# Slot mixture: ScalarE's copy of the turned dispatch weights placed before the combination exponential and the copy of the normalised slots

## What is computed

```python
# h: [16 batches, 192 tokens, 192], phi: [64 experts, 16 slots, 192]
xn = unit(h)                                   # normalised tokens
logits = einsum('bmd,npd->bmnp', xn, phi)
dispatch = softmax(logits, over the tokens m)  # a slot's weights over tokens
combine  = softmax(logits, over the slots np)  # a token's weights over slots
slots = einsum('bmnp,bmd->bnpd', dispatch, h)
slots = layernorm(slots) * ln_g[n] + ln_b[n]
y = gelu(slots @ w1[n] + b1[n]) @ w2[n] + b2[n]
h = h + einsum('bmnp,bnpd->bmd', combine, y)
```

## Time and profile before

| | |
|---|---|
| median of 3 runs | 2569.57 us |
| the runs | 2563.82, 2569.94, 2569.57 us |
| the profiled execution | 2563.13 us, its span 2561.2 us |
| mean granted clock of TensorE | 0.942 of full |
| slot stages (`first`, three `both`), from the first logits to the last copy of rows | 1904 to 1983, 2054 to 2142, 2211 to 2297, 2366 to 2454 us |

### The profile page before, as it was taken

How to read it: one execution, slowest core, us unless ns; L and a number is a source line. 1 busy time by engine, 2 the same in 40 slices (tenths; PEclk the granted TensorE clock), 3 DMA queues, 4 the chain that set the end, 5 groups by cost and what they waited for, 6 DMA issues and landing times. The chain is left out here.

```text
span 2561.2 us, 52598 instructions
## 1 busy us (share of the span) xinstructions
PE 2327.5 (91%) x18199; PEld 2047.2 (80%) x18199; DVE 1322.8 (52%) x3939; ACT 870.8 (34%) x2148; POOL 517.4 (20%) x616
## 2 busy tenths in 40 slices
PE   9968999997994899997999879999787999999997
PEld 9957999996873789996888667777557888888986
DVE  3663333335997211113888635655577264472744
ACT  2411222224881233332333213433344343342430
POOL 1223322322432444431222110000021010010100
PEclk9979999998995899999999867999889999999999
DMA  3124455611102686662000000000002633527265
GB/s 117 29 64 134 143 163 156 181 53 45 51 25 63 198 239 207 205 177 59 20 19 1 10 4 6 7 7 9 12 15 63 178 95 103 167 56 201 73 160 157
DMA packets 234545, 235.02 MB, mean 92 GB/s; under 512 B 29736, under 2 KB 214942, under 8 KB 234270
## 3 DMA queue, kind: packets, MB, share of 16 engines
q1 hardware_dynamic: 220638, 203.56, 28.5%
q0 software_dynamic: 11520, 27.54, 3.4%
q10 hardware_dynamic: 2240, 1.99, 0.3%
HBM read 277.77 MB, written 35.45 MB: 122 GB/s over the span
## 5 line engine op out<-in xcount | busy, mean ns | idle before, releaser
L572 PE MATMUL f_pg<-f_vxT,f_w 128*128 128x128 f32 x2112 | 260.7, 278 | 3.1 <-DVE f_vxT L642 3.1
L572 PEld LDWEIGHTS f_pg<-f_vxT,f_w 128*128 128x128 f32 x2112 | 256.1, 195 | 4.6 <-DVE f_vxT L642 4.6
L584 PE MATMUL f_po<-f_wd,f_hid 128*128 128x192 f32 x1440 | 254.3, 326 | 1.2 <-DVE f_vout L668 0.7
L584 PEld LDWEIGHTS f_po<-f_wd,f_hid 128*128 128x128 f32 x1440 | 231.2, 190 | 2.0 <-issue 1.7
L545 POOL DMA_INDIRECT f_answers<-f_vout,f_to_row x120 | 118.5, 987 | 422.8 <-DVE f_vout L666 250.6
L653 DVE TENSOR_TENSOR f_hid<-f_silu,f_pg 128x128 f32<-128x128 f32 x336 | 81.8, 284 | 207.1 <-ACT f_silu L621 191.8
L621 ACT ACTIVATE f_silu<-f_pg 128x128 f32<-128x128 f32 x336 | 78.5, 277 | 292.5 <-PE f_pg L578 272.7
L626 ACT ACTIVATE f_hid<-f_pg,f_b 128x128 f32<-128x128 f32 x384 | 106.3, 375 | 196.0 <-PE f_pg L578 196.0
L578 PE MATMUL f_pg<-f_vxT,f_wr 64*128 64x128 f32 x2112 | 151.1, 285 | 0.0
L2565 POOL TENSOR_TENSOR s_small<-s_small,s_half 128x2 f32<-128x2 f32 x64 | 44.4, 693 | 504.6 <-DVE s_small L2892 504.6
L578 PEld LDWEIGHTS f_pg<-f_vxT,f_wr 64*128 64x128 f32 x2112 | 128.0, 188 | 14.7 <-issue 0.4
(11 more groups left out here) (412 smaller groups left out, 4854.0 us busy)
## 6 DMA issues: line engine op xcount, KB each, us to landing
f_wd<-in_L_ffn_W SPq DMA_DIRECT2D x64, 576.0 KB
f_wd<-in_L_ffn_WdT SPq DMA_DIRECT2D x56, 576.0 KB
f_w<-in_L_ffn_W SPq DMA_DIRECT2D x64, 384.0 KB
f_w<-in_L_ffn_WgT SPq DMA_DIRECT2D x56, 384.0 KB
f_w<-in_L_ffn_WuT SPq DMA_DIRECT2D x56, 384.0 KB
s_w<-in_w SPq DMA_DIRECT2D x64, 288.0 KB, 3.7
f_wr<-in_L_ffn_W SPq DMA_DIRECT2D x128, 96.0 KB
s_w<-in_w SPq DMA_DIRECT2D x64, 192.0 KB, 4.2
```

Of the source, the lines that this page charges most:

```text
L572: pe.matmul(pg[j][:, a * ROWS:(a + 1) * ROWS], lift[a][r][:, j * 128:j * 128 + 128], xT[r][:, 0, :], start=(a == 0), stop=False, skip_grou ...
L584: last = pe.matmul(po[:, 0:D], hid[r][:, j, :], wd[r][:, j, :], start=(at == 0), stop=(at == FC - 1))
```

## The change

In each iteration b of `batches`, ScalarE copied the turned dispatch weights of batch b last. Now it copies them right after the dispatch exponential of b+1, before the combination exponential of b+1 and the copy of the normalised slots of b−2. No instruction, wait or buffer is added, removed or altered; `batches` serves `first` and all three `both` stages.

```diff
                 for b in range(B + 2):
                     if b + 1 < B:
                         exp_disp(n, b + 1)
+                    if b < B:
+                        keep_disp(n, b)
+                    if b + 1 < B:
                         exp_combine(n, b + 1)
                     if b >= 2:
                         keep_rows(n, b - 2)
-                    if b < B:
-                        keep_disp(n, b)
```

## The result

The changed kernel took 2557.17 us (median of 6 runs, 2554.42 to 2559.68), the kernel before 2569.0 us (median of 6 runs, 2563.82 to 2577.02). The ratio is 0.9949, 95% interval 0.9931 to 0.9966: 0.51% faster, some 13 us (the two medians are 11.8 us apart). The forecast was 2562.3 us within 2554.5 to 2569.0, and 7.3 us less, 4.6 to 9.3 by its own bounds: the time fell inside the range, and the saving above those bounds. The profiled execution has a span of 2552.3 us, against 2561.2.

The account below looks back on a forecast made before the run. DVE and GpSimd were taken to bound `first`, a two-batch loop through ScalarE and the token DMA the `both` stages. Savings of 1.2 + 1.7 + 2.25 + 2.1 = 7.3 us off 2569.57 gave 2562.3 us, range 2554.5 to 2569.

Parts of the forecast that it names:

- `first` is bound by DVE and GpSimd, its gap on TensorE counts for nothing: In the body of `first`, DVE sets 4.18 us a batch; closing TensorE's 0.44 us gap gains 0; contrary rival 4%.
- End of `first`: Slots of batch 14, at the stage's end, start 0.90 us earlier; gain 1.2 us, bounds 0.9 to 2.3.
- Two-batch loop in `both`: In `both`, the weighing-token-exponentials-copy loop falls from 9.81 to 8.91 us, below TensorE's 4.79 a batch: gains 0.9, 1.1, 0.8.
- Second loop over DVE, with 0.3 us of room for the token: In `both`, token DMA, DVE's normalising and turned slots take 9.2 us per two batches, under 9.58; rival it binds: 13%.
- Heads and ends of the `both` stages: At `both` stage starts gains of 0.4, 0.4 plus 0.25, and 0.8 us; at their ends 0.4, 0.5 and 0.5.
- Cover behind the copy: After the turn, copy, exponential and rows' copy take 1.5 us while TensorE has 2.6 us of work: 1.1 us spare.
- Sum: 1.2 us for `first` plus 1.7, 2.25 and 2.1 for the three `both` stages: 7.3 us, bounds 4.6 to 9.3.
- if the stages shorten and the expert stages grow: Named sign that the forecast is wrong: slot stages get shorter but the expert stages get longer; no size given.
- The chances: For the whole run: over 0.3% faster 40%, within 0.3% 54%, slower 6%.

Follow-up runs that it names:

- before_extra: Kernel before with one more ScalarE instruction per batch, a copy of the combination weights ahead of their exponential, so ahead of the dispatch copy; ratio 1.0054.
- after_long: Changed kernel with two long ScalarE copies (96x1200 each) per batch between the dispatch copy and the combination exponential; ratio 1.0246.
- half: Kernel before with the dispatch copy moved ahead of the rows' copy only, still behind the combination exponential; ratio 0.9979.
- before_tokfirst: Kernel before with SP issuing each token DMA in `both` one batch earlier, ahead of the answers' DMA; ScalarE's order untouched; ratio 0.9977.
- after_extra: Changed kernel with one more ScalarE copy of the combination weights per batch, standing behind the dispatch copy; ratio 0.9965.
- after_tokfirst: Changed kernel with SP issuing each token DMA in `both` one batch earlier, ahead of the answers' DMA; ratio 0.9950.
- after: The changed kernel itself in the first comparison against the kernel before; median 2557.17 us, ratio 0.9949.
- again: The changed kernel measured a second time, on another occasion, against the kernel before; ratio 0.9963.
- null: The kernel before, unchanged, run under another label against itself; ratio 1.0006.

## Why the prediction held, point by point

- *`first` is bound by DVE and GpSimd, its gap on TensorE counts for nothing:* right. 4.18 to 4.19 us a batch with either order in every kernel but before_extra and after_long, and the gap went behind the slots. The rule of the Trainium skill that points to the engine with the highest occupancy (Perfetto Trace Analysis, Identifying the Most-Contended Engine) would have given 5.3 us more here; the trace did not agree.
- *End of `first`:* 1.2 us predicted, 1.4 by the means, but in part by luck. The turned slots waited for DVE as said. The clock was not as I had taken it: I summed that end at the lower level, as if the drop would stay. In the five kernels with the old order in `first` (before_extra apart) and in half, a stretch at the lower level began 0.1 to 0.7 us after the slots of batch 14 had started; in none of the six with the new order was there one at that place. From the statistics of batch 13 to those of batch 15 it is 8.86 us in the kernel before and 6.78 in the changed one: 2.1 us gained, near the upper bound of 2.3 (its terms give 2.4). Of that 0.45 is lost again, since the last turned slots now fall into the next stretch at the lower level (1.11 us for 0.66). So the copy's place also moved the clock here. Why the stretch begins where it does, no run shows.
- *Two-batch loop in `both`:* right, and shown from four sides: before_tokfirst stretches it over three batches and gets 4.79 with the old order; before_extra lengthens it and gets 5.11 where 5.11 was computed; half takes 0.49 off and finds the same floor; after_extra has nothing in it. Inside the stages I had 0.9 + 1.1 + 0.8 = 2.8 us; the means over three kernels each, 4.957 to 4.823 us a batch, give 0.134 × 24 = 3.2.
- *Second loop over DVE, with 0.3 us of room for the token:* right as to place: turned slots of 0.46 to 0.59 us in the chain where DVE was late, gone inside the stages with after_tokfirst. Its length of 9.2 us was 0.2 too short. Bare in the changed kernel it is 9.61 with a token of 3.31 us, so 9.39 with one of 3.09, and the room is 0.2: the add takes 0.56 there and not 0.47, and the turned slots with their hand-over 0.70 and not 0.6.
- *Heads and ends of the `both` stages:* 0.8 to 1.3 a stage predicted, 3.25 in all; 6.4 − 3.2 = 3.2 by the means. In single profiles they scatter: the first stage gained 3.5 us and not 1.7, where the traces show that its token of batch 3 landed 6.16 us after its issue and not 6.75, and that a stretch of lower clock at its end was not there.
- *Cover behind the copy:* the sign was right (after_extra), the size too large: 0.8 us and not 1.1.
- *Sum:* 7.3 us for the four stages. By the same means 1.4 + 6.4 = 7.8 us; by the single profiles 6.96 (after) and 7.5 (again).
- *A sign of being wrong that showed:* I had named "if the stages shorten and the expert stages grow". In the first profile they did, by 3.1 us. In again the expert stages take 208.1 us, less than the 209.0 before, so the profiles show no cost handed on to them.
- *The whole run:* here the sum was short of the ratio. 7.8 us would be 0.9970. The first comparison gave 0.9949 with 0.9966 as its upper end, the second, on another occasion, 0.9963 with 0.9945 to 0.9981. The mean of the two is 0.9956, or 11 us, of which some 3 are found in no slot stage. My own bounds, 4.6 to 9.3 us, hold neither of the two savings (13 and 9.5 us); that 2557.17 us lies in the range comes from the scatter of the runs that I had put into it. The start of `first` alone moves by 16 us between executions of identical code, and null came out at 1.0006.
- *Whether that is scatter:* the surplus comes back. From old to new order the runs differ by 23 us with the additional instruction, 7 with SP's order and 9 with six buffers, and the four stages by 19.7, 3.1 and 1.2. Only the last surplus, 7.8 us, is larger than the intervals of its two ratios allow (some 7 us), and each stage sum is one profile. In the profiles, all that follows the start of `first` outside the slot stages takes 317.6 us in the mean of six kernels with the old order in `both` and 315.7 with the new one. In part this is the clock in the first expert stage: 4.4 to 4.5 us at the lower level in five of the six kernels with the new order in `first` (11.1 in after), 6.0 to 10.2 in half and the six with the old one. So something outside the slot stages may gain too, and how much of the 3 us is that and how much scatter stays open.
- *The chances:* I gave 40% to more than 0.3% faster and 54% to less. It came out faster, on the side that I held less likely. What I undervalued was the upper side: the `both` stages before run at 4.90 to 5.01 us a batch from one execution to the next, and the profile that I worked from lay at the low end.

## What to carry to other kernels

Write the stage as loops and compare their lengths. An instruction in the wrong place on an idle engine costs only where it lies on the longest loop, and moving it pays only down to the next one: here from 4.90–4.97 to 4.79, no further, whether 0.49 or 0.90 us were taken off, and another edit to the same loop (SP's order) made the move worthless inside the stages. Where an engine serves several others in turn, let it serve the one that is late first, and work out what then stands in its queue behind a wait.

## What I had not expected of the hardware

The clock that TensorE is granted makes more noise than the change has effect. In identical code ahead of `first` the time at the lower level went from 252.6 to 286.7 us between executions, and the start of the stage from 1899.1 to 1913.7. The change itself moved such a stretch too, at the end of `first`. A stage's own time, from one profile, tells a change of 7 us well, where the medians of 12 runs beside 23 still leave an interval of 9 us.

Two ScalarE copies of 96x1200 from float32 to bfloat16 took 2.19 us on the chain, so about 1.1 each, where I had estimated 0.85. A straight line through the profile's 0.52 us for 384 elements a partition and 0.59 for 512 would have given 0.97.
